# A gated cross-attention block with a low-rank linear layer: the mean of x as a column beside the probabilities in place of a centred W, and another order of loads and casts in the first tile

## The chip, the cores and the metric

The kernel runs on one core of a Trainium2 chip. The metric is the device time of one execution in microseconds. The core has five engines with queues of their own: TensorE (PE, matrix products into PSUM; PEld is its load of stationary operands), VectorE (DVE), ScalarE (ACT), GpSimd (POOL) and SyncE (SP), which here only issues DMAs. They meet through semaphores alone. Each engine runs its own queue in the order of the program.

## What is computed

```python
# x (4, 2048, 512), ctx (4, 77, 512), W (512, 512), rank 4; gates g_xattn, g_ffn
def layernorm(x): m = mean(x); v = var(x); return (x - m) / sqrt(v + 1e-5)

s  = layernorm(x) @ ctx.T                      # per batch, 77 scores per row
x1 = x + tanh(g_xattn) * softmax(s) @ ctx
L  = up_aux @ (lora_up @ (lora_down @ down_aux))
out = x1 + tanh(g_ffn) * (layernorm(x1) @ (W + L).T + b)
```

## The kernel before

**Tiles.** The 4 x 2048 rows of x are 64 tiles of 128 rows (T = 64, TB = 16 per batch). A unit is two tiles; one DMA loads a unit of x (x_sb, 512 KB, load_x) and one its transposed copy, which the host lays out (xt_raw, 512 KB, load_xt). The rings hold eight tiles. All products are kept near fp32 precision: every operand is split in a rounded high part and a low part (the rest), and three products of parts are added.

**The algebra.** PE multiplies the transposed tile xT (high part by ACT, x_hi, low part by POOL, x_lo) with wc, which holds for each of four chunks of 128 inputs the columns of the gated W + L, transposed, and beside them the 77 columns of the centred context. So one pass gives both y = x W and the scores. x1 = x + p @ ctx is never multiplied with W itself: the context is multiplied with W once per batch (cw_ps), and p @ (ctx W) is added to y in PSUM. Both row blocks, ctx and ctx W, with high and low parts, stand in "stacks", 1024 columns wide, and the transposed probabilities pT, again in parts, are the stationary operand. Since layernorm takes the mean of x1 away, each row of W must have mean zero; **before, W and dn_st (one factor of L) are centred ahead of the loop** (w_centre L847 to L855 on DVE for quarters 0 and 3, w_mean L530 with L408 on POOL and L550 on ACT for quarters 1 and 2; w_cent). PE then transposes 128x128 blocks of w_cent (w_transpose L683) into the banks of y_ps and adds the low-rank product (L705); ACT casts the result to wc's high part with the gate tg as scale (L555), DVE makes the low part (L872), and PE forms the first context product (first_product L594).

**A tile's step.** On PE (step L649): three products of chunk 0 for the half that holds the scores, the transpose of the last tile's probabilities (p_transpose L619), the rest of that half, half of the other one, the last tile's product with the stacks (p_product L624: a_ps for x1, then y), the rest. DVE takes the maximum of the scores (maxima), the reciprocal (inverse), x1 (x1_rows), the statistics of the tile two ahead (row_stats L751), the low part of pT (p_lo L792) and the output (output L802). ACT does exp (exponents L476), x_hi of the tile two ahead, the probabilities (p_ext, written twice side by side, L489), the squares of x1 (variance L492), and pT's high parts (p_hi L470). POOL adds the bias (L384), computes both inverse deviations (rs, L398 and L400) and x_lo of the tile two ahead (L372).

**The start.** SP issues low_in, two quarters of W, waits until the last quarter of W is there, then x's first unit, b_row, the three copies of the context's rows to the stacks (stack_hi, after v_hi from ACT, L434), xt's second unit, x's second unit, the copies of the low rows (stack_lo), first_stack_lo (L282), and the further units. ACT issues the context, low_out, W's other two quarters and xt's first unit. POOL makes bias_g from b_row (L392) between x_lo(0) and the first rs.

## Time and profile before

| | |
|---|---|
| three runs | 308.57 us median, 308.13 to 308.93 |
| profiled execution | 308.33 us |
| its span, first to last instruction | 306.5 us |
| PE busy | 297.7 us, 97% |
| PE weight loads | 283.8 us, 93% |
| DVE busy | 233.1 us, 76% |
| POOL busy | 226.5 us, 74% |
| ACT busy | 186.9 us, 61% |
| DMA | 56.37 MB, mean 184 GB/s |

The span leaves out 1.8 us around the execution. Shares of busy time are means over the span: in the first slice of 40 (7.7 us) PE is at six tenths, from the second to the last but one at nine or more. The page's chain of waits gives PE 95% of the span.

### The profile page before, as it was taken

The numbers are of one execution on the slowest core, as the hardware profiler recorded it, in microseconds if no ns is written. First come the engines' busy times: TensorE is split into PE (matmuls) and PEld (weight loads), VectorE is DVE, ScalarE is ACT, GpSimd is POOL, SyncE is SP. The second block draws the span as 40 slices with busy tenths as digits, with TensorE's granted clock in tenths as the row PEclk, the third lists the DMA queues.
The fourth block names the chain that finished last, engine by engine and source line by source line (L and its number), as shares of the span: only waits on it lengthen the run. The fifth ranks groups of instructions, "written<-read, shape, count | busy, mean of one in ns | idle before, by whom it ended". The sixth has DMA issues, their size and how long they took to land.

```text
span 306.5 us, 6443 instructions
## 1 busy us (share of the span) xinstructions
PE 297.7 (97%) x2070; PEld 283.8 (93%) x2070; DVE 233.1 (76%) x737; ACT 186.9 (61%) x545; POOL 226.5 (74%) x276
## 2 busy tenths in 40 slices
PE   6999999999999999999999999999999999999992
PEld 4689999999999999999899999999999999999992
DVE  3877777895787877798587787778777787778755
ACT  2856566754576656666476665657665665657652
POOL 3757787788487778777578777887778777877763
PEclk9999999999999999999999999999999999999997
DMA  7854554345585495565176579544445555443103
GB/s 206 267 206 173 197 206 160 150 166 192 185 260 190 167 248 212 207 205 208 48 205 210 205 222 288 200 154 163 166 172 207 206 207 204 175 161 149 43 28 137
DMA packets 16557, 56.37 MB, mean 184 GB/s; under 512 B 2073, under 2 KB 2073, under 8 KB 16524
## 3 DMA queue, kind: packets, MB, share of 16 engines
q1 hardware_dynamic: 15944, 54.65, 52.8%
q10 hardware_dynamic: 580, 1.32, 1.2%
q8 instruction: 16, 0.26, 0.4%
q14 instruction: 17, 0.14, 0.1%
HBM read 35.84 MB, written 16.78 MB: 172 GB/s over the span
## 4 chain that ended last, share of the span: by engine, by line
PE 95%; DMA 1%; DVE 1%; ACT 1%; issue 0%; POOLq 0%; POOL 0%; ACTq 0%; DVEq 0%
PE y_ps L613 67%; PE a_ps L639 10%; PE y_ps L644 10%; PE y_ps L621 2%; PE c_ps L589 2%; DMA low_in_sb<-in_low_in 1%; PE y_ps L684 1%; PE a_ps L571 1%; PE y_ps L689 1%; PE a_ps L601 1%; PE c_ps L580 0%; PE a_ps L605 0%; PE y_ps L705 0%; PE y_ps L566 0%; DVE o_sb L813 0%
## 5 line engine op out<-in xcount | busy, mean ns | idle before, releaser
L613 PE MATMUL y_ps<-wc,xT 128*128 128x334 f32 (+1 forms) x1536 | 227.6, 302 | 0.1
L613 PEld LDWEIGHTS y_ps<-wc,xT 128*128 128x128 f32 x1536 | 213.6, 189 | 2.1 <-issue 0.3
L384 POOL TENSOR_TENSOR x_bias<-x,bias_g 128x512 f32<-128x512 f32 x63 | 81.5, 1294 | 59.7 <-DVE x L775 59.7
L372 POOL TENSOR_TENSOR xT<-xt_raw,xT 128x512 fp32r<-128x512 f32 x64 | 82.9, 1295 | 0.1
L482 ACT ACTIVATE expd<-y_ps,neg_max,rs 128x77 f32<-128x77 f32 x64 | 26.6, 416 | 80.5 <-DVE neg_max L765 80.5
L496 ACT ACTIVATE squares<-x,x_nmean 128x512 f32<-128x512 f32 x64 | 46.4, 726 | 16.4 <-DVE x_nmean L783 16.4
L400 POOL TENSOR_TENSOR rs<-stat_eps,half_neg 128x2 f32<-128x2 f32 (+1 forms) x67 | 46.2, 689 | 5.2
L813 DVE SCALAR_TENSOR_TENSOR o_sb<-y_ps,rs,x_bias 128x512 f32<-128x512 f32 x64 | 48.0, 750 | 1.4 <-issue 0.8
L644 PEld LDWEIGHTS y_ps<-stacks,pT 109*128 109x128 f32 (+1 forms) x256 | 39.5, 191 | 5.3
L754 DVE BATCH_NORM_STATS2 bn<-x_sb 128x6 f32<-128x512 f32 x64 | 43.8, 685 | 0.0
L775 DVE SCALAR_TENSOR_TENSOR x<-a_ps,x_sb 128x512 f32<-128x512 f32 x64 | 43.7, 682 | 0.2 <-PE a_ps L639 0.2
L644 PE MATMUL y_ps<-stacks,pT 109*128 109x256 f32 (+1 forms) x256 | 40.7, 281 | 0.0
L639 PE MATMUL a_ps<-stacks,pT 109*128 109x512 f32 (+1 forms) x128 | 40.2, 395 | 0.0
L467 ACT ACTIVATE xT<-xt_raw 128x512 fp32r<-128x512 f32 x63 | 39.2, 622 | 0.0
L796 DVE TENSOR_TENSOR pT<-y_ps,pT 13x128 fp32r<-13x128 f32 x62 | 18.0, 291 | 27.8 <-ACT pT L473 27.8
L762 DVE TENSOR_REDUCE s_max<-y_ps 128x1 f32<-128x77 f32 x64 | 15.0, 234 | 23.5 <-PE y_ps L613 23.4
L489 ACT ACTIVATE p_ext<-expd,e_inv 128x154 f32<-128x154 f32 x64 | 26.5, 414 | 1.0 <-DVE e_inv L790 0.9
L473 ACT ACTIVATE pT<-y_ps 96x128 fp32r<-96x128 f32 x62 | 16.7, 269 | 5.8 <-PE y_ps L621 5.6
L639 PEld LDWEIGHTS a_ps<-stacks,pT 109*128 109x128 f32 (+1 forms) x128 | 19.7, 190 | 0.2 <-issue 0.2
L799 DVE TENSOR_TENSOR pT<-y_ps,pT 64x128 fp32r<-64x128 f32 x62 | 17.5, 283 | 1.9
L474 ACT ACTIVATE pT<-y_ps 64x128 fp32r<-64x128 f32 x62 | 16.7, 269 | 1.5
L621 PE MATMUL y_ps<-ident,p_ext 128*96 128x128 f32 x62 | 16.8, 271 | 0.5 <-ACT p_ext L489 0.5
(82 smaller groups left out, 183.9 us busy)
## 6 DMA issues: line engine op xcount, KB each, us to landing
x_sb<-in_x SPq DMA_DIRECT2D x32, 512.0 KB, 4.2
xt_raw<-in_xt SPq DMA_DIRECT2D x31, 512.0 KB, 5.1
out<-o_sb SPq DMA_DIRECT2D x31, 512.0 KB, 3.0
stacks<-v_hi SPq DMA_DIRECT2D x2, 308.0 KB
w_all<-in_w ACTq DMA_DIRECT2D x2, 256.0 KB, 6.4
xt_raw<-in_xt ACTq DMA_DIRECT2D x1, 512.0 KB, 7.3
stacks<-v_hi SPq DMA_DIRECT2D x2, 256.0 KB
stacks<-v_lo SPq DMA_DIRECT2D x2, 256.0 KB
```

Of the source, the lines that this page charges most:

```text
L372: pool.tensor_tensor(xT[:, k % TRING, 1, :, :], xt_raw[:, k % XRING // UNIT, k % UNIT, :, :], xT[:, k % TRING, 0, :, :].bitcast(F32), ALU. ...
L384: pool.tensor_tensor(x1_bias[:, q, :], x1[:, j, :], bias_g[:, :], ALU.add).then_inc(x1b_ready, 1)
L400: pool.tensor_tensor(rs[:, q, a:b], stat_eps[:, q, a:b], half_neg[:, a:b], ALU.pow).then_inc(rs_ready, 1)
L467: act.activation(xT[:, k % TRING, 0, :, :], xt_raw[:, k % XRING // UNIT, k % UNIT, :, :], ACT.Copy)\
L482: act.activation(expd[:, j, 0:V], scores(k), ACT.Exp, bias=neg_max[:, j:j + 1], scale=rs[:, k % 4, 0:1], accum_out=e_sum[:, j:j + 1]).then ...
L496: act.activation(squares[:, k % 2, :], x1[:, k % 2, :], ACT.Square, bias=x1_nmean[:, k % 2:k % 2 + 1], scale=D ** -0.5, accum_out=stat[:, ...
L613: mm = pe.matmul(y_half(k, h)[:, 0:n], xT[:, k % TRING, part, c, :], wc[:, c, w, h * H:h * H + n], start=(c == 0 and part == 0 and w == 0) ...
L639: mm = pe.matmul(a_ps[:, :], pT[0:rows[s], k % 2, s, :], stacks[0:rows[s], pair, s, 0:D], start=(s == 0), stop=(s == 1))
L644: mm = pe.matmul(y_half(k, h)[:, 0:H], pT[0:rows[s], k % 2, s, :], stacks[0:rows[s], pair, s, D + h * H:D + (h + 1) * H], start=False, sto ...
L754: dve.bn_stats(bn[:, k % 2, :], x_sb[:, k % XRING, :]).then_inc(bn_ok, 1)
L775: dve.scalar_tensor_tensor(out=x1[:, j, :], in0=a_ps[:, :], scalar=1.0, in1=x_sb[:, k % XRING, :], op0=ALU.mult, op1=ALU.add, accum_out=x1 ...
L813: dve.scalar_tensor_tensor(out=o_sb[:, q, :].rearrange("p (h d) -> p h d", h=2), in0=y_both(k), scalar=rs[:, (k + 3) % 4, 1:2], in1=x1_bia ...
```

## The change

**W is not centred.** The host lays W out by input chunk (w_part), and PE transposes the blocks of each chunk as soon as its quarter lands, then adds the low-rank product of that chunk. w_cent, its statistics and the sums on ACT are gone; dn_st is a plain copy of the product.

**The mean as a column.** Row 0 of the first batch's context is a row of zeros with its gate set to one (tg_row), and the identity's column is added in c_cent, so that row 0 of the context's transposed block is all ones; its product with W gives the column sums of W. Row 0 of the stacks holds (0, column sums) for all batches. ACT writes minus the mean of x into p_ext's first column in every tile (L494), the probabilities follow. So the stacks have 110 rows where they had 109, and two small DMAs copy row 0 to the other stack after the first tile (stack_row0).

**Order.** xt's first unit comes as two halves, the first on ACT's queue with its own semaphore. SP issues three quarters of W, x's first unit, the second half, and xt's second unit without a wait in between; then the stack copies, x's second unit, b_row. The scores' columns of wc are written by ACT (high) and DVE (low), before by POOL. On PE the first tile's scores and the first context product are woven (first_scores), and eight products on the zeroed tile expd stand at the start where five on the identity did. ACT casts v_hi after W; in tile 0 first_product_hi stands between exp and p_ext, the stack's copies behind p_ext. bias_g is made after the statistics of tile 1.

```diff
-            sp.wait_ge(ld_w[KC - 1], 16)
+            load_w(sp, 2)
+            load_w(sp, 3)
             load_x(0, 0)
-            sp.dma_start(b_row[:, 0:D], b.partition_broadcast(P)).then_inc(ld_b, 16)
+            load_x0t(1, ld_xt[0])
+            load_xt(1, 1)
             sp.wait_ge(zeroed, 1)
             sp.wait_ge(v_hi_ok, 1)
             stack_hi(0, 0, slice(0, D))
-            sp.wait_ge(ld_x[0], 16)
-            load_xt(1, 1)
             load_x(1, 1)
+            sp.dma_start(b_row[:, 0:D], b.partition_broadcast(P)).then_inc(ld_b, 16)
             sp.wait_ge(v_lo_ok, 1)
...
             for k in (-2, -1):
                 step(k, k)
+            pool.wait_ge(ld_b, 16)
+            pool.tensor_scalar(bias_g[:, :], b_row[:, 0:D], tg[:, 1:2], None, ALU.mult).then_inc(biasg_ok, 1)
             all_tiles(step, prep)
...
             def probabilities(t, k):
 
                 j = k % 2
+                act.wait_ge(mv_ready, t + 1)
+                act.activation(p_ext[:, j, 0:1], stat[:, k % 4, 0:1], ACT.Copy, scale=-1.0).then_inc(p_ready, 1)
                 act.wait_ge(inv_ready, t + 1)
-                act.activation(p_ext[:, j, :].rearrange("p (a v) -> p a v", a=2), twice(k), ACT.Copy,
+                act.activation(p_ext[:, j, 1:1 + 2 * V].rearrange("p (a v) -> p a v", a=2), twice(k), ACT.Copy,
                                scale=e_inv[:, j:j + 1]).then_inc(p_ready, 1)
...
             for c in range(KC):
                 act.wait_ge(w_tr, c + 1)
                 act.activation(wc[:, c, 0, 0:D], w_bank(c), ACT.Copy, scale=tg[:, 1:2]).then_inc(w_hi_ok, 1)
+            ctx_rows_hi(0)
             x_hi(1, 1)
-            first_product_hi()
             all_tiles(step, prep)
...
+            def first_scores():
+
+                pe.wait_ge(xl_ready, 1)
+                pe.wait_ge(c_cols, 2)
+                pe.wait_ge(ct_lo_ok, 1)
+                for c in range(KC):
+                    pe.wait_ge(w_hi_ok, c + 1)
+                    for part in range(2):
+                        pe.matmul(y_half(0, 1)[:, 0:H + VP], xT[:, 0, part, c, :], wc[:, c, 0, H:H + H + VP],
+                                  start=(c == 0 and part == 0), stop=False, skip_group_check=True)
+                        cw_part(c, part, 0)
+                    pe.wait_ge(w_lo_ok, c + 1)
+                    mm = pe.matmul(y_half(0, 1)[:, 0:H + VP], xT[:, 0, 0, c, :], wc[:, c, 1, H:H + H + VP],
+                                   start=False, stop=(c == KC - 1), skip_group_check=True)
+                mm.then_inc(s_ready, 1)
+                for c in range(KC):
+                    mm = cw_part(c, 0, 1)
+                mm.then_inc(cw_mm, 1)
...
+            def w_transposes(c):
+                pe.wait_ge(ld_w[c], 16)
+                for o in range(KC):
+                    pe.matmul(w_bank(c)[:, o * P:(o + 1) * P], w_part[:, c, o, :], ident[:, :],
+                              is_transpose=True, start=(o == 0), stop=False, skip_group_check=True)
...
                 dve.scalar_tensor_tensor(out=wc[:, c, 1, 0:D], in0=w_bank(c), scalar=tg[:, 1:2],
                                          in1=wc[:, c, 0, 0:D].bitcast(F32), op0=ALU.mult, op1=ALU.subtract)\
                     .then_inc(w_lo_ok, 1)
-            row_stats(0, 0)
+                if c == 2:
+                    row_stats(0, 0)
+            ctx_rows_lo(0)
```

SP's queue at the start, before and after. The row L232 or L231 is a unit of x, L236 or L235 a unit of its transposed copy.

```order
L232 DMA x_sb<-in_x 128x1024
L307 DMA b_row<-in_b 128x512
L248 DMA stacks<-v_hi 77x512
L248 DMA stacks<-v_hi 13x512
L248 DMA stacks<-v_hi 64x512
L236 DMA xt_raw<-in_xt 128x1024
L232 DMA x_sb<-in_x 128x1024
```

```order
L231 DMA x_sb<-in_x 128x1024
L314 DMA xt_raw<-in_xt 128x512
L235 DMA xt_raw<-in_xt 128x1024
L247 DMA stacks<-v_hi 78x512
L247 DMA stacks<-v_hi 14x512
L247 DMA stacks<-v_hi 64x512
L231 DMA x_sb<-in_x 128x1024
L328 DMA b_row<-in_b 128x512
```

The bias row went from in front of the three copies to behind them, the second unit of the transposed copy the other way; x's second unit stays behind them.

POOL's queue from tile 0's cast to the low part of tile 2, before and after. The three rows L372 or L384 are x_lo of tiles 0, 1 and 2.

```order
L411 CAST xT<-xt_raw 128x512
L372 TENSOR_TENSOR xT<-xt_raw,xT 128x512
L364 CAST wc<-ct 128x4x77 x2
L392 TENSOR_SCALAR bias_g<-b_row,tg 128x512
L398 TENSOR_TENSOR stat_eps<-stat,eps 128x1
L400 TENSOR_TENSOR rs<-stat_eps,half_neg 128x1
L372 TENSOR_TENSOR xT<-xt_raw,xT 128x512
```

```order
L415 CAST xT<-xt_raw 128x512
L384 TENSOR_TENSOR xT<-xt_raw,xT 128x512
L405 TENSOR_TENSOR stat_eps<-stat,eps 128x1
L407 TENSOR_TENSOR rs<-stat_eps,half_neg 128x1
L384 TENSOR_TENSOR xT<-xt_raw,xT 128x512
L405 TENSOR_TENSOR stat_eps<-stat,eps 128x1
L407 TENSOR_TENSOR rs<-stat_eps,half_neg 128x1
L419 TENSOR_SCALAR bias_g<-b_row,tg 128x512
L405 TENSOR_TENSOR stat_eps<-stat,eps 128x1
L407 TENSOR_TENSOR rs<-stat_eps,half_neg 128x1
L384 TENSOR_TENSOR xT<-xt_raw,xT 128x512
```

The bias product moved from behind x_lo of tile 0 to behind that of tile 1, still in front of tile 2's.

ACT's queue ahead of the loop, before and after. L555 or L559 are the casts of W, L434 or L439 is v_hi.

```order
L445 ACTIVATE ct<-c_ps 128x4x77
L533 ACTIVATE w_cent,w_nmean<-w_all 128x512
L544 ACTIVATE tg<-w_all 128x2
L434 ACTIVATE v_hi<-c_rows,tg 77x512
L547 ACTIVATE up_st<-y_ps 68x512
L533 ACTIVATE w_cent,w_nmean<-w_all 128x512
L550 ACTIVATE w_cent<-w_all,w_nmean 128x512
L555 ACTIVATE wc<-y_ps,tg 128x512 x4
```

```order
L548 ACTIVATE up_st<-y_ps 68x512
L450 ACTIVATE ct<-c_ps 128x4x78
L551 ACTIVATE wc<-ct 128x4x77
L553 ACTIVATE tg<-w_all 128x2
L555 ACTIVATE tg_row<-tg 128x1
L559 ACTIVATE wc<-y_ps,tg 128x512 x4
L439 ACTIVATE v_hi<-c_rows,tg 78x512
```

v_hi moved from in front of up_st and the casts of W to behind them.

## Rows read from the trace of the kernel before

**Rows 1.** The chain of waits by time: start us, us, what (line, count).

```profile
7.55 1.90 PE y_ps L689 x2
...
11.36 0.85 PE y_ps L684 x4
...
13.04 0.22 PE y_ps L684 x2
13.26 0.23 PE y_ps L705
...
21.05 0.32 ACT p_ext L489
...
21.73 2.11 PE y_ps L613 x15
23.84 0.46 PE a_ps L639 x2
...
25.93 0.11 PE y_ps L621
```

**Rows 2.** PE by time at the start: start us, us, line, operation, idle before.

```profile
1.58 2.51 PE L566 MATMUL y_ps<-ident 128*128 128x128 f32 x10 [1.58 <-POOL ident L355]
5.06 1.97 PE L571 MATMUL a_ps<-low_in_sb 100*68 100x512 f32 x2 [0.97 <-DMA low_in_sb<-in_low_in]
```

**Rows 3.** Busy us of each engine from 100 to 200 us, clock, DMA.

```profile
100.00:200.00 100.00, 100.00 (x715) 96.83 (x714) 78.32 (x255) 62.62 (x188) 76.14 (x90) 1.00 0.63 202
```

**Rows 4.** ACT by time, 8 to 15.5 us.

```profile
8.38 0.42 ACT L445 ACTIVATE ct<-c_ps 128x308 fp32r<-128x308 f32 x1
...
9.30 0.19 ACT L544 ACTIVATE tg<-w_all 128x2 f32<-128x2 f32 x1
9.59 0.72 ACT L434 ACTIVATE v_hi<-c_rows,tg 77x512 fp32r<-77x512 f32 x1
10.22 0.57 ACT L547 ACTIVATE up_st<-y_ps 68x512 fp32r<-68x512 f32 x1
...
13.08 2.42 ACT L555 ACTIVATE wc<-y_ps,tg 128x512 fp32r<-128x512 f32 x4 [0.92 <-PE y_ps L705]
```

**Rows 5.** DVE by time, 10 to 16.5 us.

```profile
10.82 0.68 DVE L864 TENSOR_TENSOR up_st<-y_ps,up_st 32x512 fp32r<-32x512 f32 x1
...
11.94 1.71 DVE L720 SCALAR_TENSOR_TENSOR v_lo<-c_rows,tg,v_hi 77x512 fp32r<-77x512 f32 x1
13.80 2.73 DVE L872 SCALAR_TENSOR_TENSOR wc<-y_ps,tg,wc 128x512 fp32r<-128x512 f32 x4 [0.15 <-ACT wc L555]
```

**Rows 6.** POOL by time, 14 to 24 us.

```profile
14.32 1.57 POOL L392 TENSOR_SCALAR bias_g<-b_row,tg 128x512 f32<-128x512 f32 x1
...
21.74 0.19 POOL L398 TENSOR_TENSOR stat_eps<-stat,eps 128x1 f32<-128x1 f32 x1
22.01 0.55 POOL L400 TENSOR_TENSOR rs<-stat_eps,half_neg 128x1 f32<-128x1 f32 x1
22.52 1.29 POOL L372 TENSOR_TENSOR xT<-xt_raw,xT 128x512 fp32r<-128x512 f32 x1
```

**Rows 7.** SP's queue by time: the three stack copies.

```profile
10.40 2.30 SPq L248 DMA_DIRECT2D stacks<-v_hi  x3
```

**Rows 8.** DMA issues, KB, us to landing (w_all by 2.2 us, b_row at 9.0).

```profile
w_all<-in_w ACTq DMA_DIRECT2D x2, 256.0 KB, 6.4
...
b_row<-in_b SPq DMA_DIRECT2D x1, 256.0 KB, 3.6
```

**Rows 9.** All engines by time in tile 1, 24.5 to 28 us.

```profile
24.61 0.41 ACT L489 ACTIVATE p_ext<-expd,e_inv 128x154 f32<-128x154 f32 x1
...
25.26 0.73 ACT L496 ACTIVATE squares<-x,x_nmean 128x512 f32<-128x512 f32 x1 [0.24 <-DVE x_nmean L783]
...
26.71 0.28 DVE L799 TENSOR_TENSOR pT<-y_ps,pT 64x128 fp32r<-64x128 f32 x1
...
27.99 0.62 PE L639 MATMUL a_ps<-stacks,pT 109*128 109x512 f32 x2
```

More of the change, by code:

```diff
@@ L251, in stack_hi @@
             def stack_hi(n, at, cols):
-                copy(n, slice(0, V), 0, v_hi, at, cols)
-                copy(n, slice(96, K0), 0, v_hi, at + Q, cols)
-                copy(n, slice(0, Q), 1, v_hi, at, cols)
+                lead = 1 if n else 0
+                copy(n, slice(lead, VP), 0, v_hi, at, cols)
+                copy(n, slice(96, K0), 0, v_hi, at + Q - lead, cols)
+                copy(n, slice(lead, Q), 1, v_hi, at, cols)
             def stack_lo(n, at, cols):
-                copy(n, slice(V, V + R), 0, v_lo, at + Q, cols)
@@ L260, in stack_lo, with stack_row0 @@
-                copy(n, slice(Q, P), 1, v_lo, at, cols)
+                lead = 1 if n else 0
+                copy(n, slice(VP, VP + R), 0, v_lo, at + Q - lead, cols)
+                copy(n, slice(Q + lead, P), 1, v_lo, at, cols)
+            def stack_row0():
+                sp.wait_ge(first_hi, 2)
+                sp.wait_ge(first_lo, 1)
+                sp.wait_ge(stacked[0], stack_landed(0))
+                for at, part in ((0, slice(0, 2)), (Q, slice(1, 2))):
+                    sp.dma_start(stacks[at:at + 1, 1, part, :].bitcast(F32), stacks[at:at + 1, 0, part, :].bitcast(F32))\
+                        .then_inc(stacked[1], 16)
@@ L273, in stack_rest @@
-                copy(n, slice(Q, V), 0, v_hi, Q - TAIL, both)
-                copy(n, slice(96, K0), 0, v_hi, Q - TAIL, both)
-                copy(n, slice(TAIL, Q), 1, v_hi, 0, both)
-                copy(n, slice(V, V + R), 0, v_lo, Q - TAIL, both)
-                copy(n, slice(Q + TAIL, P), 1, v_lo, 0, both)
+                rest = Q - 1 - TAIL
+                copy(n, slice(1 + TAIL, Q), 0, v_hi, 0, both)
+                copy(n, slice(Q, VP), 0, v_hi, rest, both)
+                copy(n, slice(96, K0), 0, v_hi, rest, both)
@@ L279, in first_stack_lo @@
+                copy(n, slice(1 + TAIL, Q), 1, v_hi, 0, both)
+                copy(n, slice(VP, VP + R), 0, v_lo, rest, both)
+                copy(n, slice(Q + 1 + TAIL, P), 1, v_lo, 0, both)
             def first_stack_lo():
                 sp.wait_ge(v_lo_ok, 2)
-                sp.dma_start(stacks[V:V + R, 0, 0, D:2 * D].bitcast(F32), v_lo[Q:V, D:2 * D].bitcast(F32))\
+                sp.dma_start(stacks[VP:VP + R, 0, 0, D:2 * D].bitcast(F32), v_lo[Q:VP, D:2 * D].bitcast(F32))\
                     .then_inc(stacked[0], 16)
@@ L507, in step @@
                     exponents(t, k)
+                if t == 0:
+                    first_product_hi()
+                    probabilities(t, k)
+                    first_product_copies()
                 if real(t + 2):
                     x_hi(t + 2, k + 2)
-                if real(t):
+                if real(t) and t:
                     probabilities(t, k)
@@ L565, in stay_busy @@
                 for _ in range(count):
-                    pe.matmul(y_ps[:, 0, 1, 0:P], ident[:, :], ident[:, :], start=True, stop=True)
+                    pe.matmul(y_ps[:, 0, 1, 0:P], expd[:, 0, 0:P], expd[:, 0, 0:P], start=True, stop=True)
+            pe.wait_ge(expd_ok, 1)
+            stay_busy(8)
             pe.wait_ge(ident_ok, 4)
-            stay_busy(5)
             pe.wait_ge(ld_in, 16)
@@ L690, in _ @@
                 .then_inc(low_mm, 1)
[L691 to L699 removed]
+            prep(0, TURN)
+            w_transposes(0)
             pe.wait_ge(dn_ok, 1)
             pe.wait_ge(up_ok, 1)
[L702 to L707 removed]
+            low_rank(0)
+            for c in range(1, KC):
+                w_transposes(c)
+                low_rank(c)
             all_tiles(step, prep, T - 1)
```

213 lines of the change are left out of this document (88 added, 125 removed).

## The prediction

> **What bounds the kernel now.** I read the windows first: between 100 and 200 us TensorE (PE) is busy 100.00 of 100 us [rows 3], and the timeline of one tile shows where every other engine stands against it [rows 9]. The chain of waits then gives the period: the first product with the probabilities' transpose runs at 23.84 us, and 15 products with W and the scores take 2.11 us [rows 1]; the same product comes again at 27.99 us [rows 9], so a tile costs 4.2 to 4.3 us of PE. From 21.4 us on PE does not stop. What the change does to the time is therefore the shift of the start of that stream, unless it makes some other engine slower than PE in the steady part.
>
> The start has a mark: the three products ahead of tile 1's transpose belong to tile 2. That transpose is at 25.93 us and one of its 334-column products takes 2.11 / 15 = 0.14 us, so **tile 2 starts at 25.93 - 3 x 0.14 = 25.5 us** [rows 1]. I forecast where that start goes.
>
> In front of it three things are slow. PE idles until the identity is made (1.58 us) and 0.97 us more for low_in [rows 2]. The transposes of W wait for centred rows: the last six run only from 11.36 us [rows 1]. And PE's clock is low: four transposes take 0.85 us (0.21 each) at 11.36 us, but two take 0.22 us (0.11 each) at 13.04 us, and a 512-column product then takes 0.23 us, the 2.4 GHz level; before it is 1.2 GHz [rows 1]. The column of granted clock prints 1.00 from the first slice on, as in the steady part [rows 3], so for the start I go by these durations. The step up at about 12.4 us came while PE had worked without a pause since 5.06 us.
>
> **Part 1, W not centred.** Gone are two bn_stats, bn_aggr and subtract on DVE, three passes with sums on ACT and one on POOL. PE transposes W as it lands. What PE waits for next is the small product's split: up_st on ACT (0.57 us) [rows 4] and its low part on DVE (0.68 us) [rows 5]. Going by the centre case of the clock below: low_in starts at 5.06 us as before, since DMA sets it, and takes 1.97 us [rows 2]; low_out takes 1.90 us [rows 1], a little less with the step inside it, to 8.7 us; ACT and DVE make up_st's two parts by 8.7 + 0.57 + 0.68 = 9.95 us; the context's and W's first transposes lie beside this. Then 0.23 us for the first low-rank product and 3 x (4 x 0.11 + 0.23) = 2.0 us for the others [rows 1]: **W transposed at 12.2 us**, against 14.4 us before, where the first context product follows.
>
> ACT, in order, does up_st (to 9.3), ct (0.42), the score columns (a copy of like size, 0.45), tanh (0.19), the gate's copy (0.19) [rows 4], with the waits between to about 10.6 us, then four casts of W, 2.42 / 4 = 0.6 us each [rows 4], to 13.0 us. It is ACT, not PE, that sets the pace here.
>
> **Part 2, the order of the loads.** The last quarter of W lands later. ACT's two quarters, issued by 2.2 us, landed after 6.4 us [rows 8], the last at about 8.6 us. Now SP's ring holds low_in and three quarters, and half of a unit of x's transposed copy stands beside them on ACT's, 256 KB more in front; at 0.3 MB/us, which is what 1.5 MB by 8.6 us from a start near 3 us comes to, that is 0.8 us: 9.4 us. It is needed at about 11.5 us, so this costs nothing; under an early clock it is needed at 10 us and still costs nothing. The Trainium skill (DMA: Bandwidth & Descriptors, "Queues, rings and completion order") says that each DMA engine takes turns between the rings of SP and ACT, which speaks against a long SP ring beside a short one; by it the last quarter would land between 9 and 9.5 us, and the sum is the same.
>
> x's second unit for the transposed copy is now ahead of the stack copies, but x itself (load_x(1, 1)) and the bias row are behind them, and v_hi, which releases the copies, moved behind the four casts of W: from 9.59 us [rows 4] to 13.0 + 0.72 = **13.7 us**. SP needs 2.30 us to issue the three copies [rows 7], 0.4 for x; b_row is issued at 16.5 us and lands 3.6 us later [rows 8], with the copies' data in front at **20.2 us**. Before, it was issued at 9.0 and there at 12.6 us [rows 8].
>
> **Part 3, POOL's order.** The centring (1.7 us) and the score columns are gone, so x_lo(0) ends at about 11.0 us. But bias_g stays in front of x_lo(2), and it now waits for b_row: bias_g 1.57, sum and power of the third tile 0.27 + 0.55, x_lo(2) 1.29 us [rows 6]: 20.2 + 1.6 + 0.8 + 1.3 = **24.0 us, when tile 2 can start**. Queued behind that wait are all of POOL's later steps, and PE waits for x_lo(2). That is 25.5 - 24.0 = **1.5 us earlier**.
>
> **Part 4, PE's own path.** Scores and context product are woven: from 12.2 us, 12 x 0.14 + 8 x 0.23 = 3.5 us: scores of tile 0 at 15.7 us; four more at 0.23 and 12 of 256 columns at 0.11 and three of 334: 18.4 us. Softmax beside it: DVE is at v_lo until 16.5 us, then maximum, statistics of tile 1, reciprocal, ACT's column and p_ext (0.4 us, as the chain has it with 0.32 at 21.05 us [rows 1]): 19.0 us. So PE stops 0.6 us, as it did before. Then 9 x 0.14 + 6 x 0.11 = 1.9 us; the product needs the low part of the probabilities, late because ACT now does the stack's copies and x_hi(2) after p_ext: 21.7 us. With 0.93 us for the product and 0.65 us more, tile 2 could start at 23.3 us. POOL's path is 0.7 us later and decides; PE's alone would give 2.2 us.
>
> v_lo took 1.71 us with POOL at work beside it [rows 5]; the bound from the other side is the four casts of the same kind, 2.73 / 4 = 0.68 us each [rows 5]. I take 1.71, since POOL is to be at x_lo(1) then; with 0.7 PE's path gains 0.6 us and the sum stays. The Trainium skill (SBUF — State Buffer, "Who interferes with whom") has the reason: a DVE instruction with two SBUF inputs contends with a GpSimd instruction that reads SBUF. By it either the 1.71 stays or POOL's x_lo(1) is held, at most 1 us, which ends before bias_g's wait in any case.
>
> **Part 5, the column in every tile.** ACT copies one column more per tile. No row has 128x1; bounds are tanh's 128x2 with 0.19 us [rows 4] and p_ext's 0.41 us [rows 9], nearest to the first. It sits ahead of p_ext. ACT idles 0.24 us between p_ext and the squares [rows 9], which takes it in. Even at 0.41 the low part, done at 26.71 + 0.28 = 26.99 us for a product at 27.99 us [rows 9], has 1.0 us in hand. Cost 0; a gain is excluded, as nothing in the steady part is removed. The matmul's 110 rows for 109, 78 context rows for 77 and SP's two small copies after tile 0 lie under the same cover.
>
> **The sum.** Profiled run 308.33 us, its span 306.5, median of the runs 308.57. With -1.5: 306.8 for the profiled one, **307.1 us** as the median.
>
> **The clock** is the term I can't take from a row, since PE now starts on the zeroed tile (at 1.15 us) and does eight products of about 0.43 to 0.50 us (five took 2.51 us [rows 2]), so that it works without a pause into low_in. The start of unbroken work moves from 5.06 to 1.15 us, by 3.9 us. If the step up moved as far, it would come near 8.5 us: my centre. The rows don't say that it moves so. The other cases:
>
> - **Early and kept (0.25).** The step comes at 5.5 to 7 us already. low_in and low_out lose 0.6 to 1.3 us, and all after it: tile 2 at 22.8 to 23.4 us, gain 2.1 to 2.7, about **306.2 us**. For it: the pause of 0.97 us is gone. Against: PE worked 1.58 to 4.09 us and from 5.06 us, and still had to go on to 12.4 us.
> - **No earlier than before (0.22).** Step at 12.5 us: up_st's parts 10.0, W transposed 13.5, casts 14.2, v_hi 14.85, b_row 21.4, tile 2 at 25.2 us: gain 0.3, **308.3 us**. For it: from 5.06 to 9 us PE does the same products as before, all of them at the low level then, and it now pauses near 9.5 us for up_st, where two products on the identity used to fill.
> - **Later (0.04).** With that pause the step comes after 13.2 us: v_hi up to 1 us later, loss 0.1 to 0.7, **309.1 us**.
> - **The bias row isn't the limit (0.07).** b_row lands sooner or the copies issue faster; PE's path holds: 2.2 us at the centre, 3.5 with an early clock, **306.4 to 305.1 us**.
> - **The column is on the path (0.04), the slower side.** ACT's longer step would delay p_ext, squares and the probabilities' transpose until PE waits each tile. The point: the 0.24 of idle time and the 1.0 us in hand, 1.2 us per tile. Only a column (with its wait on the statistics) above that costs, the excess times 62 tiles: at 1.3 us, 6 us, **315 us**. Against: tanh's 0.19 us.
> - **Centre (0.38)**: 307.1, from 306.6 to 307.7 us.
>
> **Numbers.** 0.3% is 0.93 us, about what a measurement can tell from no change. The centre, the early clock and the free bias row are beyond it, save the upper edge of the centre (0.05): faster 0.65. Late clock and that edge within: same 0.31. Slower 0.04. The range from 305.2 to 308.6 us leaves out the column, the later clock and a corner of the best case.
>
> **What would show it.** Two transposes of W in 0.22 us by 9 us: early clock. PE's first wait after the start on up_st; bias_g starting at about 20.2 us on a DMA, and PE waiting for x_lo(2) at 22 to 24 us. In the steady part PE busy 100%, period unchanged, ACT's idle time before the squares smaller. Wrong if tile 2 starts before 22 us (b_row or the clock misjudged), if DVE waits long for x's second unit ahead of the low part, or if PE idles in the steady part.

## The result and the profile after

| | before | changed |
|---|---|---|
| median of 15 runs each | 308.64 us | 309.62 us |
| lowest, highest | 308.03, 310.82 | 309.14, 312.51 |
| profiled execution, its span | 308.33, 306.5 | 312.28, 310.5 |
| tile 1's transpose starts at | 25.77 | 28.17 |
| steady time per tile | 4.314 us | 4.345 us |

The changed kernel is slower: ratio 1.0054, 95% interval 1.0032 to 1.0077. Predicted were 307.1 us and a range from 305.2 to 308.6. Nine of its 15 runs lie at 309.1 to 310.0 us, one at 310.7, four at 312.3 to 312.5 and one at 311.7; the profiled one is of the upper group, which has to be kept in mind below.

I use two measures from here on. The first is when tile 1's transpose starts (tile 2's stream begins three products ahead of it); on the timeline of PE it stands at 25.77 us before. The second is the steady time per tile: the mean distance of two transposes with one whole tile's instructions between them, the context's steps left out. The coarse form of it can be read off the summary of the transposes' line: count, ns of one (least, middle, most), first and last start. Before, then changed:

```profile
L621 PE MATMUL y_ps<-ident,p_ext x62: 270/270/315, 21.4 to 291.0; 128*96 128x128 f32 x62
```

```profile
L635 PE MATMUL y_ps<-ident,p_ext x62: 270/270/272, 21.1 to 295.2; 128*96 128x128 f32 x62
```

From tile 1 to tile 61 that is 291.0 - 25.8 = 265.2 us before and 295.2 - 28.2 = 267.0 us after. **The profiled execution's 4.0 us of longer span are 2.4 us at the start and 1.8 us in the steady part;** the end is 0.2 to 0.3 us shorter.

**The steady part.** PE is as busy as in [rows 3], and that row shows nothing of it:

```profile
100.00:200.00 100.00, 100.00 (x710) 96.74 (x709) 77.63 (x253) 64.34 (x209) 76.02 (x89) 1.00 0.60 199
```

The time is in the six products with the stacks. By shape, from 45 to 290 us, before and then changed (line, operation, shapes, count, busy us, mean ns of one):

```profile
L644 PE MATMUL y_ps<-stacks,pT 109*128 109x256 f32 x112 | 28.9, 281 | 0.0
L644 PE MATMUL y_ps<-stacks,pT 128*128 128x256 f32 x112 | 28.9, 280 | 0.0
L639 PE MATMUL a_ps<-stacks,pT 109*128 109x512 f32 x56 | 22.1, 395 | 0.0
L639 PE MATMUL a_ps<-stacks,pT 128*128 128x512 f32 x56 | 22.1, 394 | 0.0
```

```profile
L658 PE MATMUL y_ps<-stacks,pT 128*128 128x256 f32 x110 | 29.0, 284 | 0.0
L658 PE MATMUL y_ps<-stacks,pT 110*128 110x256 f32 x110 | 29.0, 284 | 0.0
L653 PE MATMUL a_ps<-stacks,pT 128*128 128x512 f32 x55 | 21.9, 399 | 0.0
L653 PE MATMUL a_ps<-stacks,pT 110*128 110x512 f32 x55 | 21.8, 397 | 0.0
```

A product of 256 columns goes from 280 or 281 to 284 ns, one of 512 from 394 or 395 to 397 or 399. The products with wc take 281 ns as before (256 columns) and 324 for 323 (334 columns). The column itself does what was expected: it takes 0.19 us on ACT and fills the idle time that stood before the squares in [rows 9].

```profile
31.33 0.19 ACT L494 ACTIVATE p_ext<-stat 128x1 f32<-128x1 f32 x1
...
31.98 0.72 ACT L503 ACTIVATE squares<-x,x_nmean 128x512 f32<-128x512 f32 x1
```

**The start.** PE by time; these rows answer to [rows 1, 2]:

```profile
4.95 1.94 PE L576 MATMUL a_ps<-low_in_sb 100*68 100x512 f32 x2
7.08 1.97 PE L711 MATMUL y_ps<-low_out_sb 50*68 50x512 f32 x2 [0.18 <-DMA low_out_sb<-in_low_out]
...
12.38 1.06 PE L703 MATMUL y_ps<-ident,w_all 128*128 128x128 f32 x4
13.09 0.78 PE L707 MATMUL y_ps<-up_st,dn_st 68*128 68x512 f32 x1
13.66 0.88 PE L703 MATMUL y_ps<-ident,w_all 128*128 128x128 f32 x4
14.30 0.48 PE L707 MATMUL y_ps<-up_st,dn_st 68*128 68x512 f32 x1
...
24.80 0.70 PE L653 MATMUL a_ps<-stacks,pT 110*128 110x512 f32 x2 [1.31 <-DVE pT L820]
...
27.60 0.73 PE L604 MATMUL y_ps<-wc,xT 128*128 128x334 f32 x3 [0.92 <-POOL xT L384]
28.17 0.27 PE L635 MATMUL y_ps<-ident,p_ext 128*96 128x128 f32 x1
```

The pause before low_in is gone, and yet the clock is low to 14.2 us: a product of 512 columns with four transposes takes 1.27 us until then (12.38 to 13.66), half of it later. SP's copies wait for v_hi on ACT, and x's second unit and b_row are queued behind them. The first row is ACT's, the next three are SP's queue, the last is the piece of the chain of waits, from issue to landing:

```profile
15.40 0.71 ACT L439 ACTIVATE v_hi<-c_rows,tg 78x512 fp32r<-78x512 f32 x1
```

```profile
16.20 2.34 SPq L247 DMA_DIRECT2D stacks<-v_hi  x3
18.59 0.59 SPq L231 DMA_DIRECT2D x_sb<-in_x  x1
19.23 0.45 SPq L328 DMA_DIRECT2D b_row<-in_b  x1
```

```profile
19.23 4.61 DMA b_row<-in_b
```

On POOL that landing releases bias_g, and x_lo(2) ends just as PE's products of tile 2 start at 27.60 us (0.92 us of idle time in PE's row above). These rows answer to [rows 6]:

```profile
17.06 1.57 POOL L384 TENSOR_TENSOR xT<-xt_raw,xT 128x512 fp32r<-128x512 f32 x1
...
23.93 1.57 POOL L419 TENSOR_SCALAR bias_g<-b_row,tg 128x512 f32<-128x512 f32 x1 [3.20 <-DMA b_row<-in_b]
...
26.28 1.27 POOL L384 TENSOR_TENSOR xT<-xt_raw,xT 128x512 fp32r<-128x512 f32 x1
```

DVE waits 0.84 us for x's second unit, in front of the probabilities' low part, and PE idles 1.31 us until 24.80 us. The row of PE names that low part (pT, L820) as the releaser, but it was done at 24.06 us. The product also needs the last copy of the first context product's low rows to the stacks (L293), which SP issued at 21.16 us, again behind x and b_row. SP's copies of row 0 (L269) wait for the landing of the same copy, and they start at 24.67 us. So some 0.7 us of the 1.31 are x's second unit's, by way of DVE, and the rest is this copy's.

```profile
16.75 0.73 DVE L733 SCALAR_TENSOR_TENSOR v_lo<-c_rows,tg,v_hi 78x512 fp32r<-78x512 f32 x1
...
22.52 0.69 DVE L775 BATCH_NORM_STATS2 bn<-x_sb 128x6 f32<-128x512 f32 x1 [0.84 <-DMA x_sb<-in_x]
...
23.78 0.28 DVE L820 TENSOR_TENSOR pT<-y_ps,pT 64x128 fp32r<-64x128 f32 x1
```

```profile
21.16 0.77 SPq L293 DMA_DIRECT2D stacks<-v_lo  x1
...
24.67 1.23 SPq L269 DMA_DIRECT2D stacks<-stacks  x2
```

### The profile page after: what moved, and what is told of

Read it like the earlier page. It is cut to its first block, busy times and chain, and to the rows that moved or that the text cites. A ratio compares the mean times of both kernels' runs of the same rounds, so it can differ in the third digit from the quotient of the medians.

```text
span 310.5 us, 6505 instructions
## 1 busy us (share of the span) xinstructions
PE 301.3 (97%) x2072; PEld 286.8 (92%) x2072; DVE 230.1 (74%) x733; ACT 191.2 (62%) x604; POOL 224.1 (72%) x274
## 4 chain that ended last, share of the span: by engine, by line
PE 92%; DMA 3%; POOL 1%; SPq 1%; DVE 1%; ACT 0%; issue 0%; ACTq 0%; POOLq 0%; DVEq 0%
PE y_ps L604 66%; PE y_ps L658 10%; PE a_ps L653 10%; PE y_ps L635 2%; DMA low_out_sb<-in_low_out 2%; PE c_ps L594 2%; DMA b_row<-in_b 1%; PE y_ps L703 1%; SPq L247 1%; PE y_ps L711 1%; PE y_ps L707 1%; POOL bias_g L419 1%; PE c_ps L585 0%; POOL xT L384 0%; DVE o_sb L834 0%
## 5 line engine op out<-in xcount | busy, mean ns | idle before, releaser
L604 PE MATMUL y_ps<-wc,xT 128*128 128x256 f32 x1524 | 226.4, 302 | 0.9 <-POOL xT L384 0.9
L384 POOL TENSOR_TENSOR xT<-xt_raw,xT 128x512 fp32r<-128x512 f32 x64 | 83.0, 1297 | 0.1
L658 PEld LDWEIGHTS y_ps<-stacks,pT 110*128 110x128 f32 (+1 forms) x256 | 40.0, 190 | 5.8
L653 PE MATMUL a_ps<-stacks,pT 110*128 110x512 f32 (+1 forms) x128 | 40.7, 399 | 1.3 <-DVE pT L820 1.3
L658 PE MATMUL y_ps<-stacks,pT 110*128 110x256 f32 (+1 forms) x256 | 41.5, 284 | 0.0
L817 DVE TENSOR_TENSOR pT<-y_ps,pT 14x128 fp32r<-14x128 f32 x62 | 18.0, 291 | 29.6 <-ACT pT L478 29.6
L653 PEld LDWEIGHTS a_ps<-stacks,pT 110*128 110x128 f32 (+1 forms) x128 | 19.6, 190 | 1.6 <-issue 1.6
L820 DVE TENSOR_TENSOR pT<-y_ps,pT 64x128 fp32r<-64x128 f32 x62 | 17.5, 283 | 1.9
L405 POOL TENSOR_TENSOR stat_eps<-stat,eps 128x2 f32<-128x2 f32 (+1 forms) x67 | 13.2, 196 | 7.3 <-DVE stat L777 5.7
```

The lines of the kernel that those rows point to most:

```text
L384: pool.tensor_tensor(xT[:, k % TRING, 1, :, :], xt_raw[:, k % XRING // UNIT, k % UNIT, :, :], xT[:, k % TRING, 0, :, :].bitcast(F32), ALU. ...
L604: mm = pe.matmul(y_half(k, h)[:, 0:n], xT[:, k % TRING, part, c, :], wc[:, c, w, h * H:h * H + n], start=(c == 0 and part == 0 and w == 0) ...
L653: mm = pe.matmul(a_ps[:, :], pT[0:rows[s], k % 2, s, :], stacks[0:rows[s], pair, s, 0:D], start=(s == 0), stop=(s == 1))
L658: mm = pe.matmul(y_half(k, h)[:, 0:H], pT[0:rows[s], k % 2, s, :], stacks[0:rows[s], pair, s, D + h * H:D + (h + 1) * H], start=False, sto ...
```

## The experiments

All kernels but the last four of the placement table (one run each) were timed beside the kernel before, whose median was 308.4 to 308.7 us in each comparison. Since the starts scatter, I give the lowest run beside the median. The transpose's time comes from one profiled run of each kernel.

**1. Is it the column, or where the tiles lie?** Removing w_cent and the statistics, and p_ext's longer row, shifted the tensors in SBUF. In the built program pT, the stationary operand of the six slow products, starts at a multiple of 64 bytes before and at 32 bytes beyond one after; so do x1, squares, x1_bias and o_sb, and p_ext and bias_g, among others, went the other way. The stacks, xT and wc are at 32 in both. Three kernels: the changed one with a pad, the one before with the same pad, and the changed one without the column from tile 2 on, which leaves out taking the mean of x away in those tiles.

```diff
+        pad = sb("pad", [P, 1])
         pT = sb("pT", [P, 2, 2, P], F32R)
```

> The changed kernel with 32 bytes of unused memory in front of pT, so that pT, x1, squares, x1_bias and o_sb start at the same place within 64 bytes as in the kernel before (pT at 145920 instead of 145888; before 154240). Nothing else differs. Steady part of the changed kernel: 4.345 us a tile against 4.319 before, and the 0.026 us stand at the six products with the stacks. If the place of the stationary tile pT is what costs them, the period returns to 4.32 us and the runs fall by 1.6 us (median near 308.0, ratio to before near 0.998). If the 110th row, the extra ACT column or anything else of the change costs them, period and time stay: 4.345 us, 309.4 to 309.6 us.

> The kernel before with the same 32 bytes in front of pT, which takes pT from 154240 to 154272 and so off the 64-byte place. If the place of pT costs the time, the period goes from 4.319 to 4.345 us and the time up by 1.6 us, to 310.2. If it is the 110th row or the column, nothing moves: 308.6 us.

```diff
+                if first(t, 2):
                     act.wait_ge(mv_ready, t + 1)
                     act.activation(p_ext[:, j, 0:1], stat[:, k % 4, 0:1], ACT.Copy, scale=-1.0).then_inc(p_ready, 1)
```

> The changed kernel without ACT's column of minus the mean from tile 2 on (this part of the computation is left out: the mean of x is not taken away in those tiles). If the ACT instruction lengthens the tile, the period falls from 4.345 to 4.32 us and the time by 1.6 us; if it lies in ACT's idle time as I predicted, both stay within 0.1 us of the changed kernel.

Measured:

| | median | lowest | ratio | per tile |
|---|---|---|---|---|
| before | 308.66 | 307.99 | | 4.314 |
| before + pad | 310.64 | 309.90 | 1.0065 [1.0050, 1.0079] | 4.342 |
| changed | 309.62 | 309.14 | 1.0054 | 4.345 |
| changed + pad | 309.18 | 307.48 | 1.0014 [0.9989, 1.0040] | 4.320 |
| changed, no column | 311.11 | 309.35 | 1.0078 [1.0050, 1.0107] | 4.346 |

The pad makes the kernel before slower by 2.0 us and turns its 4.314 into 4.342; in the changed kernel it gives 0.025 us per tile back, and the lowest run falls by 1.7 us (the median by only 0.4, for the reason in part 3). Without the column nothing changes per tile: **ACT's instruction for the column is free, and most of the steady part's loss, 0.025 of 0.031 us per tile, is the place of the tiles.** Some 0.006 us per tile are left between 4.314 and 4.320. No experiment is on them; what the padded kernel still has of the change are the 110th row and the new places of p_ext and bias_g.

**2. The order of the loads.** With x's second unit and b_row both issued ahead of the waits for the copies, and with b_row alone so:

```diff
             load_xt(1, 1)
+            load_x(1, 1)
+            sp.dma_start(b_row[:, 0:D], b.partition_broadcast(P)).then_inc(ld_b, 16)
             sp.wait_ge(zeroed, 1)
             sp.wait_ge(v_hi_ok, 1)
             stack_hi(0, 0, slice(0, D))
-            load_x(1, 1)
-            sp.dma_start(b_row[:, 0:D], b.partition_broadcast(P)).then_inc(ld_b, 16)
```

> The changed kernel with x's second unit and the bias row issued by SP ahead of the wait for v_hi, not behind the three stack copies. In the changed kernel POOL's bias product waited until 23.93 us for the bias row and DVE until 22.52 us for x's second unit; tile 2 started at 27.6 us after 0.92 us of waiting for POOL and the first product waited 1.31 us. If these loads are the cost of the start, both waits go, POOL makes the bias product by 15 us, and the start is 2 us or more earlier (median 307.5 or below, with the longer tile period still in it). If ACT's and PE's own chains hold the start, it gains less than 1 us.

> The changed kernel with only the bias row ahead of the wait for v_hi; x's second unit stays behind the stack copies. POOL's bias product then no longer holds x_lo of tile 2 (0.92 us of waiting on PE), but DVE still waits for x's second unit before the low part of the probabilities (1.31 us on PE) and POOL for its statistics. If the bias row was the limit, as I predicted, the start gains 1.5 us or more and comes within 0.3 us of the version with both loads moved. If x's second unit holds it as much, tile 2 starts about 1 us later than in that version.

Both loads early: 309.60 us median, lowest 307.06, against 309.62 and 309.14 for the changed kernel. So the median missed the 307.5 us that I had expected, though the lowest run fell by 2.1 us; part 3 comes back to this. Its profiled run has the clock's step as late as the changed one's (13.9 us), so the two can be compared: bias_g waits for no DMA, PE has no pause from the scores on, and the transpose comes at 25.28 in place of 28.17 us. Of these 2.9 us, 0.3 stand already at tile 0's transpose (20.84 for 21.10 us); from there to tile 1's it is 4.44 us in place of 7.07.

```profile
20.45 1.57 POOL L419 TENSOR_SCALAR bias_g<-b_row,tg 128x512 f32<-128x512 f32 x1
22.44 0.19 POOL L405 TENSOR_TENSOR stat_eps<-stat,eps 128x1 f32<-128x1 f32 x1 [0.42 <-DVE stat L777]
```

```profile
23.09 0.70 PE L653 MATMUL a_ps<-stacks,pT 110*128 110x512 f32 x2
...
24.12 1.33 PE L604 MATMUL y_ps<-wc,xT 128*128 128x256 f32 x9
25.28 0.27 PE L635 MATMUL y_ps<-ident,p_ext 128*96 128x128 f32 x1
```

With b_row alone: 309.34 us, lowest 307.85, ratio 1.0029 [1.0003, 1.0056]. The step came early in its profiled run. bias_g waits no more, but x's second unit does its part: DVE waits 0.54 us for it and PE 0.38 us for pT. PE's other wait, 0.46 us at 12.24, is for x_lo of tile 0 and has nothing to do with that unit. From DVE, then PE:

```profile
19.94 0.69 DVE L775 BATCH_NORM_STATS2 bn<-x_sb 128x6 f32<-128x512 f32 x1 [0.54 <-DMA x_sb<-in_x]
```

```profile
12.24 0.42 PE L622 MATMUL y_ps<-wc,xT 128*128 128x334 f32 x1 [0.46 <-POOL xT L384]
...
18.86 2.35 PE L604 MATMUL y_ps<-wc,xT 128*128 128x334 f32 x15
21.59 0.70 PE L653 MATMUL a_ps<-stacks,pT 110*128 110x512 f32 x2 [0.38 <-DVE pT L820]
```

The transpose is at 23.78 us there; with both loads early and an early clock (the padded kernel below) it is at 22.55. Of these 1.2 us, 0.7 stand already at tile 0's transpose (18.83 and 18.10 us). So, by one profiled run of each, **the two loads behind the copies cost 2.6 us where the clock is late, x's second unit alone about 0.5 us where it is early.**

**3. Both, and the clock.** Pad and early loads together; that kernel with the start of before (five products on the identity); and the kernel before with the eight products on the zeroed tile.

> Both edits together on the changed kernel: 32 bytes in front of pT, and x's second unit with the bias row ahead of the wait for v_hi. If the two costs are separate (0.026 us a tile, and the waits at the start), they add: 1.5 us less than the version with the loads alone, so 305.5 to 306.2 us where PE's clock steps up once and for good, and about 308 us where it falls back. Median 306 to 307.5, below both kernels. If the tile's place was not the cause, it stays at the 309.6 us of the loads alone.

```diff
-            pe.wait_ge(expd_ok, 1)
-            stay_busy(8)
             pe.wait_ge(ident_ok, 4)
+            stay_busy(5)
```

> As the one with pad and loads, but PE starts as the kernel before does: five products on the identity from 1.58 us, then a pause until low_in lands, in place of eight on the zeroed tile. In one profile of the changed kernel the clock stepped up at 14.24 us; in another one of its offspring it rose at 4.22, fell at 7.63 and rose again at 14.46 us. If the eight products at the start are what makes the clock rise early and fall again, this one shows one step between 10 and 14.5 us, and its runs lie closer together (within 1.5 us) than those with eight (3.5 us). If the weak products between 5 and 9 us are what holds the clock low, the spread of the runs stays.

> The kernel before with only the start of PE as in the changed kernel: eight products on the zeroed tile from 1.2 us. If the start of PE moves the clock's step, as I predicted (from 12.4 to near 8.5 us), the kernel before gains by up to 1 us. If it makes the clock rise early and fall back, its runs spread from 308 to 310.5 us. If it does nothing, 308.6 us with the same spread as before (308.0 to 309.2).

| | median | runs | ratio | transpose, profiled |
|---|---|---|---|---|
| pad, early loads | 305.52 | 305.08 to 307.97 | 0.9922 [0.9898, 0.9946] | 22.55 |
| the same, five products | 308.01 | 307.42 to 308.34 | 0.9971 [0.9955, 0.9987] | 25.65 |
| before, eight products | 308.86 | 307.46 to 309.5 | 0.9997 [0.9979, 1.0015] | 25.59 |

The first beats both kernels. PE at its start, eight products and then five:

```profile
5.06 1.41 PE L577 MATMUL a_ps<-low_in_sb 100*68 100x512 f32 x2
6.73 1.07 PE L712 MATMUL y_ps<-low_out_sb 50*68 50x512 f32 x2 [0.25 <-DMA low_out_sb<-in_low_out]
...
9.60 0.60 PE L704 MATMUL y_ps<-ident,w_all 128*128 128x128 f32 x4
```

```profile
4.76 1.98 PE L576 MATMUL a_ps<-low_in_sb 100*68 100x512 f32 x2 [0.68 <-DMA low_in_sb<-in_low_in]
...
10.77 1.05 PE L703 MATMUL y_ps<-ident,w_all 128*128 128x128 f32 x4
```

With eight products, low_in's pair takes 1.41 us and the next pair 1.07: the step lies inside the first pair. With five, low_in's pair takes 1.98 us, four transposes still 1.05 at 10.77 where they take 0.60 above, and the transpose is 3.1 us later. So the eight products do what was hoped, with operands that are all zero: they bring the step forward by 9 us between these two runs (the traces' first record of the full clock is at 5.8 and 14.8 us), and the medians are 2.5 us apart. In the kernel before the same early step (6.9 us) gives nothing, since PE then waits for centred rows, 1.42 us on DVE and 0.83 on ACT. What the change of W's centring adds is that PE has no such wait behind the early step:

```profile
10.72 0.66 PE L685 MATMUL y_ps<-ident,w_cent 128*128 128x128 f32 x4 [1.42 <-DVE w_cent L855]
12.22 0.41 PE L685 MATMUL y_ps<-ident,w_cent 128*128 128x128 f32 x2 [0.83 <-ACT w_cent L550]
```

But the step isn't kept in every run. With the pad alone it came by 5 us and fell back about 7.6 us, after PE had stood for low_out: low_out's pair takes 1.24 us, the four transposes behind it 1.06, the low level.

```profile
6.86 1.24 PE L712 MATMUL y_ps<-low_out_sb 50*68 50x512 f32 x2 [0.76 <-DMA low_out_sb<-in_low_out]
...
8.61 1.06 PE L704 MATMUL y_ps<-ident,w_all 128*128 128x128 f32 x4
```

In the run without the column it fell back at 23.7 us, where PE stood 1.91 us in front of the stacks' products. The row names no releaser, but it is the same copy to the stacks as above: SP's copies of row 0, which wait for it, start at 23.23 us. Most of the stream up to tile 1's transpose then ran at 1.2 GHz: nine products of 256 columns take 2.31 us where they take 1.33 above.

```profile
23.35 0.91 PE L654 MATMUL a_ps<-stacks,pT 110*128 110x512 f32 x2 [1.91 <-issue]
...
24.92 2.31 PE L605 MATMUL y_ps<-wc,xT 128*128 128x256 f32 x9
27.03 0.30 PE L636 MATMUL y_ps<-ident,p_ext 128*96 128x128 f32 x1
```

The run with the pad had a pause of 1.85 us at the same product, ended by the same copy, and kept its clock. So such a pause doesn't always bring a fall.

Late steps and falls make the upper groups. Every run has its mean granted clock on record; a fall shows in it, a late step doesn't. With both loads early, seven of the eight runs over 309 us have 0.984 to 0.986 (the eighth is the profiled one, with the late step), and the four under 308 us 0.995 to 0.998. With the pad too, the three over 307 us have 0.988 to 0.991, the other seven 0.994 to 0.999. That is why an edit that gains 2 us in the lowest run can leave the median where it was. For the changed kernel the lower group can be worked out: 309.2 us is a span of 307.4 us; less 15.3 us of end and 267.0 of stream, tile 1's transpose is at about 25.1 us, 3 us before the profiled one. That is the 3.1 us between the two starts above.

**4. Filling the pause.** Two more products on the zeroed tile in front of low_out's wait, once alone and once beside the kernel without them.

```diff
+            stay_busy(2)
             pe.wait_ge(ld_out, 16)
```

> The changed kernel with the early loads and the pad (305.52 us median, 305.08 to 307.97), and two more products on the zeroed tile between low_in's product and low_out's, where TensorE stood 0.25 to 0.76 us for low_out in the runs in which the products were fast, and where one run fell back to the slow level soon after. Theory A (the pause there is what lets the clock fall back in some runs, and gives the 307.3 to 308.0 us among them): nearly all runs at 305.1 to 305.7 us, none over 307. Rival B (the moment at which the clock steps differs from run to run by itself): the same spread, 305.1 to 308 us, median 305.3 to 306.5. Rival C (in a run whose clock is late, the two products stand in front of low_out's and delay everything by 0.9 us): the upper runs at 308 to 309 us.

> The filled pause once more, on one chip with the same kernel without the two products. It gave 305.44 to 306.03 us in five runs, where three in ten of the kernel without them lay over 307 us; five runs without such a one would come with a chance of 0.7 to the fifth, 0.17, if nothing had changed. Theory A (the pause lets the clock fall back): again none over 307 us. Rival B (chance): about as many over 307 us as beside it.

305.89 us (five runs, 305.44 to 306.03), ratio 0.9908 [0.9889, 0.9927]; then 305.85 us (six, 305.41 to 307.30), 0.9928 [0.9906, 0.9950], beside 306.63 us (twelve, 305.19 to 310.14), 0.9945 [0.9922, 0.9968] without them. One run in 11 is over 307.2 us with the fill, 7 in 22 without; a split at least as good comes by chance about one time in six. The spans say more, since up to 3.5 us of a run's time here lie outside its span, where most have 1.8 to 2.1. With the fill all eleven spans are 303.3 to 304.2 us; the run of 307.30 us has 304.2. Without it seven of 22 are 305.4 to 306.7 us, six of them at a granted clock of 0.983 to 0.991. By chance a split like that comes about one time in 25; in the second comparison alone, none of six against four of twelve, one time in six. The two products cost 0.2 to 0.4 us in the lowest run, about as expected; **that they keep the clock is likely and not shown.** The fill doesn't give the lowest median: that is 305.52 us, without it.

**5. What of the place counts?** With the early loads, pads at other points moved groups of tiles between a multiple of 64 bytes (0) and 32 beyond (32). The diff is that of xT moved.

```diff
+        pad = sb("pad", [P, 1])
         xT = sb("xT", [P, TRING, 2, KC, P], F32R)
...
-        pad = sb("pad", [P, 1])
         pT = sb("pT", [P, 2, 2, P], F32R)
```

> The changed kernel with the early loads and the pad ahead of pT (its run before: 305.52 us, period of a tile 4.3197 us), and a second pad of one column behind pT. So pT stays at an address that is a multiple of 64 bytes, and x1, squares, x1_bias and o_sb move to 32 beyond one, as in the changed kernel as it was made. Theory A (the stationary operand of the six stack products is what counts): period 4.319 to 4.321 us, time 305.2 to 306.0 us. Rival B (a vector tile at 32 bytes is what counts, x1 or squares, by way of the semaphores that TensorE gets later): period 4.345 us, a_ps products 397 and 399 ns in place of 395 and 394, and 60 times 0.026 = 1.6 us longer, 306.7 to 307.5 us.

> The changed kernel with early loads, and the pad ahead of xT in place of ahead of pT: xT, the stationary operand of the 24 products with wc in each tile, moves from 32 beyond a multiple of 64 bytes to a multiple, as pT is already. Theory A (each product whose stationary tile lies at 32 costs some 4 ns more; six products gave 0.026 us per tile): 24 x 0.0043 = 0.10 us less per tile, period 4.22 us, 6 us less over the kernel, 299.5 us. Rival B (the six stack products are special, since their stationary tile is loaded once and used for 512 or 256 columns from the stacks, or since pT is written just before it is read): period 4.319 us and 305.5 us as with the pad ahead of pT alone. TensorE needs at least (9 x 512... columns) about as long as now if its columns set the time, which speaks for B.

> The changed kernel with early loads, and the pad ahead of wc: wc and the stacks (moving operands), x's rings and xT all move to multiples of 64 bytes, pT as before. Theory A (placement counts for the stationary operand alone): the same as the run with xT alone moved, within 0.005 us per tile. Rival B (the moving operand's place counts too): a period that differs from that run's by more than 0.01 us per tile, either way. If neither counts: 4.319 us and 305.5 us.

> The changed kernel with the early loads; pads put the stacks at a multiple of 64 bytes, xT and pT at 32 beyond one. The period of a tile is read. Known (stacks, xT, pT): (32, 32, 0) 4.320, (32, 32, 32) 4.345, (32, 0, 0) 4.331, (0, 0, 0) with wc at 0 too 4.352 us. Theory A (each tile's place has its own price): 4.320 + 0.026 + 0.021 = 4.366 us. Rival B (what counts is which of the three stand alike): this is the mirror of (32, 0, 0), so 4.331 us.

> Stacks and xT at a multiple of 64 bytes, pT at 32 beyond one. Theory A (own prices): 4.320 + 0.026 + 0.012 + 0.021 = 4.378 us. Rival B (which stand alike): the mirror of (32, 32, 0), the fastest: 4.320 us.

| stacks | xT | pT | per tile | if each place had its own price | time (median, or the one run) |
|---|---|---|---|---|---|
| 32 | 32 | 0 | 4.320 | | 305.52 |
| 32 | 32 | 32 | 4.346 | | 309.60 |
| 32 | 0 | 0 | 4.331 | | 306.89 |
| 0 (wc 0 too) | 0 | 0 | 4.352 | | 308.05 |
| 0 | 32 | 32 | 4.325 | 4.366 | 308.31 |
| 0 | 32 | 0 | 4.346 | 4.341 | 308.44 |
| 0 | 0 | 32 | 4.317 | 4.378 | 305.24 |
| 32 | 0 | 32 | 4.318 | 4.357 | 305.10 |

With x1, squares, x1_bias and o_sb at 32 and pT at 0 the first row stays at 4.320 us: the places of these vector tiles don't count. (That kernel's median is 307.01 us, 305.11 to 311.26; its profiled run steps at 17.3 us.) The second row is the run with early loads and no pad. The first four rows are timed kernels, and each of the seven profiles of the changed kernel with (32, 32, 0) gave 4.319 to 4.320, so 0.005 us is well outside the scatter. That the 24 products with xT gain 4 ns each by its place falls at once: 4.331 us came, and not 4.22. Own prices fall, by 0.04 to 0.06 us in three rows of four. My rival, that only it counts which of the three stand alike, has the mirrors right within 0.007 us in three pairs (first and seventh, second and fourth, third and fifth) and misses the last (4.346 against 4.318). What holds in all eight: where pT stands as the stacks do, a tile takes 4.318 to 4.352 us, where it stands otherwise 4.317 to 4.331, and of each such pair with xT kept, the unlike one is faster in three of four. Why is open; so is what the bits above 32 do, which these pads moved too. And in all eight p_ext stands where xT doesn't (at 0 where xT is at 32, and the other way), so what the table puts down to xT may be p_ext's.

## Why the prediction was wrong

**Part 5, the steady part: the step that failed.** "Cost 0; a gain is excluded, as nothing in the steady part is removed." The column's cost is 0 as said. But I priced a steady part by its instructions alone. The list of tensors is part of it: the edit to it moved pT by 32 bytes against a multiple of 64. That is worth 0.025 us per tile in the changed kernel and 0.028 in the one before, 1.5 to 1.7 us over 60 tiles; with the unexplained rest the stream is 1.8 us longer, more than the whole predicted gain. The slower side that I had priced there was a wait for the column (315 us); what came is a few ns in each of six products that no edit touches. As a sum, 309.6 - 1.8 = 307.8 us would lie inside the range. The run with the pad says that this isn't the whole miss: its lowest is 307.48 us, but its median is 309.18, outside the range, and in five of its twelve runs the mean granted clock of 0.983 to 0.988 shows a fall. The start below is the other part. The Trainium skill (TensorE: Matmul & The Clock Gate, "Step-by-step: what each phase is for") says that TensorE has two independent read ports, so that the load of the next stationary operand takes no bandwidth from a running product. No run here tests that. The traces show only that the products with the stacks take 280 or 284 ns by where the tiles lie, with pT, their stationary tile, moved among others.

**Parts 2 and 3, the bias row: right mechanism, wrong size.** bias_g does wait for b_row, then PE for x_lo(2), as forecast. From v_hi's end to the landing I had 6.5 us (13.7 to 20.2); it is 7.7 (16.1 to 23.8). The copies took 2.34 as said; x's unit took 0.6 to issue, not 0.4, and b_row 4.6 to land where the row of before, with less in front, had 3.6. From the landing on it took 3.8 us, as the sum had it.

**x's second unit and the low rows' copy: left out.** I named the first under what would make the forecast wrong and gave it no price, and the second not at all. Both stand behind the copies as b_row does. DVE waits 0.84 us for x ahead of the low part of pT, and PE stands 1.31 us in all, until the low rows' copy has landed. In the profiled run the path over b_row ends later still (PE waits another 0.92 us for x_lo(2)), so b_row decides, as forecast; but moving b_row alone would leave the other two.

**Part 1 and the clock.** v_hi ended at 16.1 us in the profiled run, not at 13.7. With a late step each quarter of W takes 1.27 us, set by PE and not by ACT, which waits 0.23 to 0.59 us before each cast. The case nearest to it, "Later", had v_hi up to 1 us behind 14.85 us and a loss of up to 0.7 us; the loss is 2.4, since v_hi ended still a little later and b_row landed 7.7 us behind it and not 6.5. The centre, a step at 8.5 us, is in none of the sixteen profiled runs of the changed kernel and its variants with eight products: they step at 4.0 to 6.9 us, keep it or lose it, or step at 13.9 us and later. "Early and kept" and "Later" were both real, and a third that I didn't have, early and lost again; they make groups of runs of one kernel. A centre between them was an average of things that happen. In the lower group, nine runs of fifteen, the gain is 0.7 us (25.8 to 25.1), where that case had 2.1 to 2.7: the copies still hold b_row and x, which I take for the reason; no run of that group is profiled.

**Part 4.** v_lo took 0.73 us and not 1.71; POOL's x_lo(1) beside it took 1.57 in place of 1.27. So the cost moved to POOL and lay in front of bias_g's wait, as the second branch had it: it changed nothing. PE's own path, with both loads early, is free of pauses from the scores on: neither the 0.6 us stop that I had before tile 0's transpose nor the wait for the low part comes.

**The sum again.** The median run is one of the lower group: -0.7 at the start where I had -1.5, and +1.8 in the steady part where I had 0: +1.1 us against 1.0 measured. Of the 2.5 us between forecast and result the steady part is 1.8, the start the rest. In the upper group the start is up to 2.4 us later than before.

## What to carry to other kernels

A change that adds or removes tensors moves all behind it; compare the tensors' addresses of both builds, and where the bound is a stream of products, time the kernel with a pad of 32 bytes before you judge the change. Where work that gates a queue moves back, everything queued behind it goes along: two loads behind the copies cost 2.6 us here. A row's releaser that was done long before the wait ended isn't what ended it; look for a landing. Warming the clock pays only where PE then has work that waits for nothing, and a clock that may step early or late, or fall, gives groups of times, not one in the middle.

## What the runs showed of the hardware that I had not expected

A 32-byte shift of a stationary operand (with the tiles behind it) changes the products with it by 0.5 to 1.4% (280 to 284 ns, 395 to 397 and 394 to 399 ns), and the effect depends on where other operands lie. Products on a tile of zeros are enough for an early step: in 13 of the 16 profiled runs with eight of them it comes at 4.0 to 6.9 us; no run has eight on other operands beside it. The clock can fall back to 1.2 GHz within a few us after it rose (up by 5, down about 7.6, up at 14.5 us in the run with the pad), and one pause of 1.9 us before 23.4 us was followed by the low level from 23.7 to 27.1 us, where another of 1.85 us was not. A run's time can hold 3 us and more outside its span (306.88 us for a span of 303.6), where most have 1.8.
